# Seven stages in one launch: first inputs loaded in the stage in front, no wait for a stage's own last stores, and another order at the lookup's ends

## The chip, the cores and the metric

One core of one Trainium2 chip runs the whole program in one launch. The metric is the device time in microseconds (us); the reference point is the median of three runs. The engines are TensorE (PE, with its weight loads as PEld), VectorE (DVE), ScalarE (ACT), GpSimd (POOL) and SyncE (SP), which here only issues transfers.

## The reference

Two layers over x of shape (2, 2048, 256) in fp32, 4096 tokens in all. Each of the four blocks is a pre-norm residual block, with `n` a layer norm without weights:

```python
x = x + mamba(n(x))      # norm, W_in (256 to 2x512), causal conv of 4, silu, B, C, delta = softplus(..)
                         # h = exp(delta*A)*h + delta*B*u over time, 16 states x 512 channels
                         # y = sum(h*C) + D*u;  residual + (y * silu(z)) @ W_out
x = x + experts(n(x))    # 16 experts; q,k,v = sum of gated expert projections, causal attention of
                         # one head of 64, its result times each gate, through o_proj
x = x + attention(n(x))  # 16 heads of 16, 4 KV heads, rotary embedding, full softmax over 2048 keys
x = x + lookup(n(x))     # top 8 of 1024 keys, softmax over them, values gathered and weighted,
                         # times a gate from log1p(variance) / mean over all tokens and a small MLP
```

The lookup's gate divides by a mean over all tokens, so no output row can be finished before the last token's variance is known.

## The kernel before

`build_program` (L2398) calls seven stages, one after the other: `mamba_front` (L104), `selective_scan` (L436), `expert_front` (L655, named moe), `causal_attention` (L1050), `rotary_front` (L1285, named rot), `full_attention` (L1542, named attn) and `key_lookup` (L1937, named look). Each opens a Scope with its own tiles and semaphores and a block with one program per engine, written out by hand: an engine runs its list in order and waits on semaphores between. What one stage hands to the next (xr, uT, gT, dT, BC, yT, x1, rwT, qkT, v0, x2, q_parts, k_parts, v1, ctx) goes through tensors in HBM.

All transfers are issued by SP and go through one hardware queue, in the order of SP's program. At the end of its program SP waits until the stage's last stores have landed. Then comes `Scope.clear` (L69): a barrier of all engines, the release of the semaphores, a second barrier. The first transfer of the next stage is issued behind it.

The 4096 tokens are 8 chunks (NCH) of 512 (CH), each of 4 tiles (TPC) of 128; a sequence has 4 chunks (CPB) or 16 tiles (QT).

- **Front.** Per chunk: norms, W_in, conv, silu into uT, the gate silu(z) into gT (ACT L333, L339), B and C rows into xdbl, softplus on ACT and POOL (L235) into dT. uT, gT and dT have one buffer each; SP stores dT of the chunk before, loads x, and stores gT, uT and BC (L153 to L188). After chunk 7 it stores dT once more and waits for all stores.
- **Scan.** SP loads unit 0 (dT, uT; 2 MB), the first quarter of b (rows of B broadcast to 128 partitions, 1 MB each), ident, the C rows, the rest of b, then unit 1. PE transposes the C rows (L630) before anything else. For each of 8 units and 16 states POOL makes du*b (L535), ACT exp(delta*A) (L559), DVE four scan operations (L594), PE and ACT the sum over states. The gated y is stored per unit.
- **moe.** Loads sim, yT, W_out, xr, ident and small inputs, then x1 = xr + y W_out (PE L976), norm, gates, 16 expert projections per chunk (PE L1000), DVE accumulation. Stores x1, rwT, v and qkT.
- **Causal.** SP loads q and k of sequence 0, masks, v, rwB (the gates of a tile of 128 queries broadcast over partitions, two transfers of 256 KB) of unit 0, w_o, rw(1), x of sequence 0, rw(2), rw(3), and all of sequence 1. rwB has 4 buffers; rw(u+4) is issued when unit u is mixed (DVE L1171). Each of 32 units is one tile of queries: scores (PE L1230), mask, softmax, transposes, values, mix with the gates (L1171), w_o and the residual (L1180). x2 is stored every four units.
- **Rot.** Norm of x2 (DVE), transposes (PE L1506), projections (PE L1516), rotary products on DVE, their sum on POOL, a split of q and k into three bf16 parts on ACT, POOL and DVE; stores v1, q_parts, k_parts. DVE does statistics, variance and normalization of a chunk ahead of its turns.
- **Attn.** POOL clears k_max, q, v and sets rows of k_exp to one (L1705 among them), DVE clears k_exp; SP loads parts between these clears. DVE takes maxima (L1787) from products on PE (L1841, L1842), then exp on ACT (L1767), values on PE (L1862). 8 pairs of sequence and KV head, 4 chunks of queries each.
- **Look.** SP loads 16 constants on one semaphore; POOL, DVE, ACT and PE all wait for all 16. PE first multiplies the router weights with the keys (rk), then x3 = x2 + ctx W_o (L2281, DVE L2035), norm, query, router scores, top 8 (MAX8, L2066), weights, `finish` (L2081) after the lookup of the values (PE L2320). `look_all` and `sum_all` hold all tokens. After the last tile DVE computes the variances, ACT Ln, PE the sum over tokens, DVE and ACT the gate (L2251), and DVE 32 results (L2166) in two buffers, which SP stores chunk by chunk (512 KB).

## Time and profile before

| what | value |
| --- | --- |
| median of 3 runs | 3662.48 us (3660.83 to 3666.27) |
| the profiled execution | 3666.12 us, of which the span 3664.1 |
| mean granted TensorE clock | 0.955 of full speed |
| busy in the span | PE 3253.3, DVE 2754.8, ACT 2232.4, POOL 964.0 us |
| transfers | 216.74 MB, mean 59 GB/s |

The stages cover, by their first and last transfers and operations: front 0 to 250, scan 255 to 910, moe 915 to 1357, causal 1360 to 1672, rot 1675 to 1812, attn 1815 to 3283, look 3286 to 3664.

A row of the timeline has the start (us from the span's start), the duration, the engine (SPq is SP's queue), the line, the operation, out<-in, shapes and count; in brackets stands the idle time of that engine before it, and who ended it. Rows of neighbouring operations of one kind are merged, with their count. A row of the windows has the stretch, its length, the busy time of PE, PEld, DVE, ACT and POOL (with counts), the granted clock PEclk, the DMA engines' busy share and the GB/s.

### The profile page before, as it was taken

The numbers are of one execution on the slowest core, as the hardware profiler recorded it, in microseconds if no ns is written. First come the engines' busy times: TensorE is split into PE (matmuls) and PEld (weight loads), VectorE is DVE, ScalarE is ACT, GpSimd is POOL, SyncE is SP. The second block draws the span as 40 slices with busy tenths as digits, with TensorE's granted clock in tenths as the row PEclk, the third lists the DMA queues.
The fourth block names the chain that finished last, engine by engine and source line by source line (L and its number), as shares of the span: only waits on it lengthen the run. The fifth ranks groups of instructions, "written<-read, shape, count | busy, mean of one in ns | idle before, by whom it ended". The sixth has DMA issues, their size and how long they took to land. (4 is left out here: it accounts for less than half of the span.)

```text
span 3664.1 us, 55043 instructions
## 1 busy us (share of the span) xinstructions
PE 3253.3 (89%) x18162; PEld 1625.8 (44%) x18162; DVE 2754.8 (75%) x4130; ACT 2232.4 (61%) x3970; POOL 964.0 (26%) x906
## 2 busy tenths in 40 slices
PE   7848888898899988997789999999999999977896
PEld 3316777776566646774312222222222222214664
DVE  6639999998566653445798888888888888835665
ACT  5659999998100001222258888888888888862442
POOL 7529999997000000002300000000000000001000
PEclk9979999999899998999879999999999999998998
DMA  4448443310311127223300000000000010011001
GB/s 132 166 139 186 124 107 93 104 58 24 107 54 45 44 44 179 70 64 102 103 14 14 21 14 21 14 21 14 21 14 21 16 24 14 9 30 46 23 23 46
DMA packets 218534, 216.74 MB, mean 59 GB/s; under 512 B 63954, under 2 KB 164434, under 8 KB 217492
## 3 DMA queue, kind: packets, MB, share of 16 engines
q1 hardware_dynamic: 218276, 213.41, 21.1%
q8 instruction: 149, 2.44, 0.3%
q14 instruction: 109, 0.89, 0.1%
HBM read 145.99 MB, written 67.37 MB: 58 GB/s over the span
## 5 line engine op out<-in xcount | busy, mean ns | idle before, releaser
L1787 DVE TENSOR_REDUCE attn_part_max<-attn_pM 128x1 f32<-128x1024 f32 x1024 | 1204.9, 1219 | 162.1 <-PE attn_pM L1842 159.0
L1767 ACT ACTIVATE attn_probs<-attn_pE 128x512 f32<-128x512 f32 x2048 | 1089.7, 597 | 205.7 <-PE attn_pE L1891 201.2
L1891 PE MATMUL attn_pE<-attn_q,attn_k_exp 128*128 128x512 bf16 x2048 | 629.0, 385 | 31.3 <-ACT attn_q L1739 24.7
L535 POOL TENSOR_TENSOR scan_dbu<-scan_du,scan_b_all 128x2048 f32<-128x2048 f32 x128 | 578.4, 4553 | 14.9 <-DVE scan_h L594 12.9
L1862 PE MATMUL attn_pA<-attn_probs,attn_v 128*32 128x512 f32 x4096 | 560.3, 604 | 0.0
L594 DVE TENSOR_TENSOR_SCAN scan_h<-scan_abar,scan_states,scan_dbu 128x512 f32<-128x512 f32 x384 | 458.6, 1301 | 0.0
L1891 PEld LDWEIGHTS attn_pE<-attn_q,attn_k_exp 128*128 128x128 bf16 x2048 | 139.1, 97 | 608.7 <-ACT attn_probs L1767 464.6
L608 PE MATMUL scan_hT<-scan_ident,scan_h 128*128 128x128 f32 x2048 | 324.1, 282 | 71.7 <-ACT scan_hcT L546 29.5
L559 ACT ACTIVATE scan_abar<-scan_delta,scan_decay 128x512 f32<-128x512 f32 x512 | 366.8, 717 | 17.3 <-DVE scan_h L594 17.3
L1720 POOL TENSOR_TENSOR attn_peak_parts<-attn_peak,attn_zero 128x4 bf16<-128x4 f32 x128 | 26.6, 208 | 1277.0 <-DVE attn_peak L1791 1277.0
L546 ACT ACTIVATE scan_hcT<-scan_hT,scan_c_t 128x512 f32<-128x512 f32 x512 | 361.7, 707 | 1.1 <-PE scan_hT L608 1.1
L1841 PE MATMUL attn_pM<-attn_k_exp,attn_q 64*128 64x512 bf16 x1024 | 325.9, 391 | 34.4 <-DMA attn_k_exp<-mid_k_parts 18.2
L1000 PE MATMUL moe_pP<-moe_w_qkv,moe_xT 128*128 128x384 f32 x1024 | 339.4, 489 | 0.9
L1842 PE MATMUL attn_pM<-attn_k_max,attn_q 64*128 64x512 bf16 x1024 | 325.9, 391 | 0.0
L618 PE MATMUL scan_y_acc<-scan_ident,scan_hcT 128*128 128x128 f32 x2048 | 303.5, 274 | 1.2 <-DVE scan_g L577 1.0
L608 PEld LDWEIGHTS scan_hT<-scan_ident,scan_h 128*128 128x128 f32 x2048 | 225.2, 143 | 168.7 <-DVE scan_h L594 113.7
L1000 PEld LDWEIGHTS moe_pP<-moe_w_qkv,moe_xT 128*128 128x128 f32 x1024 | 193.0, 191 | 131.3 <-DVE moe_acc L872 4.6
L618 PEld LDWEIGHTS scan_y_acc<-scan_ident,scan_hcT 128*128 128x128 f32 x2048 | 239.8, 142 | 4.6 <-issue 2.5
L1841 PEld LDWEIGHTS attn_pM<-attn_k_exp,attn_q 64*128 64x128 bf16 x1024 | 83.2, 93 | 304.7 <-issue 169.5
L875 DVE SCALAR_TENSOR_TENSOR moe_acc<-moe_pP,moe_rw,moe_acc 128x192 f32<-128x192 f32 x448 | 161.8, 412 | 75.1 <-PE moe_pP L1000 74.5
L594 DVE TENSOR_TENSOR_SCAN scan_h<-scan_abar,scan_dbu 128x512 f32<-128x512 f32 x128 | 150.7, 1221 | 40.5 <-POOL scan_dbu L535 37.7
L1862 PEld LDWEIGHTS attn_pA<-attn_probs,attn_v 128*32 128x32 f32 x4096 | 95.5, 108 | 146.5 <-ACT attn_probs L1767 110.7
(274 smaller groups left out, 3642.8 us busy)
## 6 DMA issues: line engine op xcount, KB each, us to landing
scan_b_all<-mid_BC SPq DMA_DIRECT2D x32, 1024.0 KB, 10.0
causal_rwB<-mid_rwT SPq DMA_DIRECT2D x64, 256.0 KB, 4.2
attn_q<-mid_q_parts SPq DMA_DIRECT2D x224, 64.0 KB, 2.4
mid_gT<-front_gT SPq DMA_DIRECT2D x8, 1024.0 KB, 7.6
mid_uT<-front_uT SPq DMA_DIRECT2D x8, 1024.0 KB, 9.2
mid_dT<-front_dT SPq DMA_DIRECT2D x8, 1024.0 KB, 4.3
scan_delta<-mid_dT SPq DMA_DIRECT2D x8, 1024.0 KB, 8.0
scan_u_in<-mid_uT SPq DMA_DIRECT2D x8, 1024.0 KB, 10.2
```

The lines of the kernel that those rows point to most:

```text
L535: nc.gpsimd.tensor_tensor(dbu[:, G % NDBU, :, :], du[:, u % 2, :, :], b_row, ALU.mult).then_inc(dbu_ready, 1)
L546: nc.scalar.activation(hcT[:, i % NHC, :], hT[:, i % 2, :], ACT.Copy, scale=c_t[:, u * TPC + tile, n:n + 1]).then_inc(hc_ready, 1)
L559: nc.scalar.activation(abar[:, k % 2, :], delta[:, u % 2, m, :], ACT.Exp, scale=decay[:, m, n:n + 1]).then_inc(abar_ready, 1)
L594: nc.vector.tensor_tensor_scan(h[:, G % NH, m, :], abar[:, k % 2, :], dbu[:, G % NDBU, m, :], state, ALU.mult, ALU.add).then_inc(scan_done, 1)
L608: last = nc.tensor.transpose(hT[:, i % 2, m * 128:(m + 1) * 128], h[:, G % NH, m, tile * 128:(tile + 1) * 128], ident[:])
L618: last = nc.tensor.matmul(y_acc[:, m, tile * 128:(tile + 1) * 128], hcT[:, i % NHC, m * 128:(m + 1) * 128], ident[:], start=(n == 0 and ti ...
L1000: last = nc.tensor.matmul(pP[:, n % NP, 0:2 * QKV], xT[:, c % 2, k, j * 128:(j + 1) * 128], w_qkv[:, k, pr * 2 * QKV:(pr + 1) * 2 * QKV], ...
L1767: nc.scalar.activation(probs[:, kt % 4, h, :], pE[:, bank(item), :], ACT.Exp, scale=SCALE).then_inc(exp_done, 1)
L1787: nc.vector.reduce_max(part_max[:, h, j, i:i + 1], pM[:, m % 2, :], AXIS_X).then_inc(max_read, 1)
L1841: nc.tensor.matmul(pM[:, m % 2, 0:CH], q[0:64, qc, h, j * 128:(j + 1) * 128], k_exp[0:64, par, i * CH:(i + 1) * CH], start=True, stop=True)
L1862: last = nc.tensor.matmul(pA[32 * h:32 * h + 32, :], v[:, par, kt, :], probs[:, kt % 4, h, :], start=(kt == 0), stop=(kt == KT - 1))
L1891: nc.tensor.matmul(pE[:, bank(item), :], k_exp[:, par, kt * 128:(kt + 1) * 128], q[:, qc, h, :], start=True, stop=True).then_inc(e_psum, 1)
```

## The change

The first inputs of six of the stages get tiles and semaphores of their own in Scopes (`scan_ahead`, `expert_ahead`, `causal_ahead`, `rotary_ahead`, `attention_ahead`, `lookup_ahead`) that are opened before the stage in front and are passed to both. The stage in front issues their loads.

- Front: at chunk 3 SP waits for three chunks' stores and loads unit 0, a_log and ident; in chunks 4 and 5 it issues two b loads each, ahead of the gT and uT stores. POOL makes du of unit 0 before its last delta. dT is now the scan's odd g tile; the last dT store is waited for in the scan, before gate 1 is loaded into it.
- Scan: starts with the C rows (now in hcT's tile), unit 1, b of unit 1, gate 0, and moe's constants. Its end waits for the even y stores only.
- moe: the first yT and xr come in two halves. At chunk 5 SP waits for the stores of chunks 0 to 4 and issues causal's first loads.
- Causal: SP waits for moe's stores, then loads x, q, k, v of the rest. In unit 17 it issues rot's first loads; DVE does chunk 0's statistics and variance in unit 22 and its normalization in unit 24; POOL the root.
- Rot: clears of attention's tiles on POOL after its add of chunks 0 to 3; attention's loads at chunks 5 and 6. DVE's clear of k_exp is gone from attn, and is POOL's.
- Attn: issues the lookup's constants at its start, and ctx and x2 of the first chunk in its last pair.
- Look: three semaphores for the constants; flips and x3 before the rk product; the gate's chain beside the last lookups, the results of chunks 0 to 3 before the `finish` of tile 30, chunks 4 to 6 before that of tile 31, chunk 7 last, in four buffers.
- No stage but the last waits at its end for its own last stores (the scan for half of them); the next one waits where it reads them.

The core of the diff:

```diff
-    def clear(self):
+    def clear(self, ahead=None):
         self.nc.all_engine_barrier()
-        self.nc.clear_and_free_semaphores(self.sems)
+        self.nc.clear_and_free_semaphores(self.sems + (ahead.sems if ahead else []))
...
+def load_scan_b(sp, a, p, u, i, b):
+    src = a["BC"][i * BQ:(i + 1) * BQ, u * CH:(u + 1) * CH]
+    sp.dma_start(b[:, i * BQ:(i + 1) * BQ, :], src.unsqueeze(0).broadcast_to([128, BQ, CH])).then_inc(p.b_in[u % 2][i], 16)
...
+                    if c == 3:
+                        for sem in (u_out, bc_out):
+                            sp.wait_ge(sem, 16 * c)
+                        sp.wait_ge(d_out, 16 * c)
+                        load_scan_unit(sp, a, following, 0, following.delta_even, following.u_even)
+                        sp.dma_start(following.a_log[:], a["a_log_d"]).then_inc(following.const_in, 16)
+                        sp.dma_start(following.ident[:], a["ident"]).then_inc(following.const_in, 16)
+                    if c in (4, 5):
+                        for i in (2 * c - 8, 2 * c - 7):
+                            load_scan_b(sp, a, following, 0, i, following.b_even)
...
-                for sem in (xr_out, u_out, g_out, bc_out, d_out):
+                for sem in (xr_out, u_out, g_out, bc_out):
...
+                    if c == NCH - 1:
+                        pool.wait_ge(following.unit_in[0], 32)
+                        nc.gpsimd.tensor_tensor(following.du_even[:], following.delta_even[:], following.u_even[:], ALU.mult).then_inc(following.du_ready, 1)
...
+        c_rows = hcT[0:NS, :, :].rearrange("p a c -> p (a c)")
...
-                sp.dma_start(a_log[:], a["a_log_d"]).then_inc(const_in, 16)
-                load_unit(0)
-                load_b(0, 0)
-                sp.dma_start(ident[:], a["ident"]).then_inc(const_in, 16)
+                    load_scan_b(sp, a, p, u, i, b_all[u % 2])
+
                 sp.dma_start(c_rows, BC[NS:2 * NS, :]).then_inc(crow_in, 16)
-                for i in range(1, 4):
-                    load_b(0, i)
                 load_unit(1)
                 for i in range(4):
                     load_b(1, i)
-                sp.wait_ge(c_psum, 1)
                 load_gate(0)
+                load_expert_ahead(sp, a, following)
+                sp.wait_ge(p.d_out, 16 * NCH)
                 load_gate(1)
                 for u in range(UNITS):
...
+                sp.wait_ge(y_out[0], UNITS // 2 * 16)
...
+def load_causal_ahead(sp, a, p):
+
+    load_qk(sp, a, p, 0)
+    sp.dma_start(p.above[:], a["above"]).then_inc(p.above_in, 16)
+    sp.dma_start(p.ident[:], a["ident"]).then_inc(p.ident_in, 16)
+    load_v(sp, a, p, 0)
+    for u in range(NRW):
+        load_rw(sp, a, p, u)
+    sp.dma_start(p.w_o[:], a["w_o"].rearrange("(m p) n -> p m n", p=128)).then_inc(p.w_in, 16)
...
+                for half, arrived in enumerate((first_in, y_in)):
+                    sp.dma_start(yT[:, :, half * 256:(half + 1) * 256], yT_view[:, :, half * 256:(half + 1) * 256]).then_inc(arrived, 16)
+                    sp.dma_start(xr[:, 2 * half:2 * half + 2, :], xr_view[:, 2 * half:2 * half + 2, :]).then_inc(arrived, 16)
...
+                        if c + 2 == NCH - 1:
+                            sp.wait_ge(p.y_out[1], 16 * NCH // 2)
                         load_y(c + 2)
+                    if c == CPB + 1:
+                        sp.wait_ge(qk_out, 16 * c)
+                        sp.wait_ge(rw_out, 16 * (c + 1))
+                        for par in range(2):
+                            sp.wait_ge(v_out[par], 16 * ((c + 1 - par) // 2))
+                        load_causal_ahead(sp, a, following)
                     store_v(c)
                 store_qk(NCH - 1)
-                for sem in (x1_out, qk_out, rw_out):
-                    sp.wait_ge(sem, 16 * NCH)
-                for sem in v_out:
-                    sp.wait_ge(sem, 16 * NCH // 2)
...
+                for sem in (p.x1_out, p.qk_out, p.rw_out):
+                    sp.wait_ge(sem, 16 * NCH)
+                for par in range(2):
+                    sp.wait_ge(p.v_out[par], 16 * NCH // 2)
                 load_x(0)
-                load_rw(2)
-                load_rw(3)
-                load_qk(1)
-                load_v(1)
+                load_qk(sp, a, p, 1)
+                load_v(sp, a, p, 1)
                 load_x(1)
                 for u in range(UNITS):
                     if u + NRW < UNITS:
-                        load_rw(u + NRW)
+                        sp.wait_ge(mix_ready, u + 1)
+                        load_rw(sp, a, p, u + NRW)
+                    if u == QT + 1:
+                        sp.wait_ge(x_out, 16 * QUARTERS)
+                        load_rotary_ahead(sp, a, following)
                     b, qt = divmod(u, QT)
                     n = QT // QUARTERS
                     if qt % n == n - 1:
                         sp.wait_ge(x_ready, u + 1)
                         sp.dma_start(x2_view[:, u + 1 - n:u + 1, :], x[:, b, qt + 1 - n:qt + 1, :]).then_inc(x_out, 16)
-                sp.wait_ge(x_out, 16 * QUARTERS * B)
+
+            @block.gpsimd
+            def _(pool):
...
+                nc.gpsimd.memset(following.mhalf[:], -0.5).then_inc(following.half_set, 1)
+                pool.wait_ge(following.half_set, 1)
+                rotary_root(nc, pool, following, 0)
...
+                    if u == QT + 6:
+                        rotary_statistics(nc, dve, following, 0)
+                        rotary_variance(nc, dve, following, 0)
+                    if u == QT + 8:
+                        rotary_normalize(nc, dve, following, 0)
                     if u:
                         add(u - 1)
...
+def clear_attention_ahead(nc, pool, p, turn):
+
+    if turn == 0:
+        nc.gpsimd.memset(p.k_max[64:128, :, :].bitcast(FP32), 0.0).then_inc(p.kmax_clear, 1)
+        pool.wait_ge(p.kmax_clear, 1)
+        nc.gpsimd.memset(p.v[:], 0.0).then_inc(p.v_clear, 1)
+        pool.wait_ge(p.v_clear, 1)
+    elif turn == 1:
+        nc.gpsimd.memset(p.q[PEAK:128, :, :, :].bitcast(FP32), 0.0).then_inc(p.q_clear, 1)
+        pool.wait_ge(p.q_clear, 1)
+    elif turn == 2:
+        nc.gpsimd.memset(p.k_exp[64:128, :, :].bitcast(FP32), 0.0).then_inc(p.kexp_clear, 1)
+        pool.wait_ge(p.kexp_clear, 1)
+    else:
+        nc.gpsimd.memset(p.k_exp[PEAK:PEAK + PARTS, :, :], 1.0).then_inc(p.ones_set, 1)
+        pool.wait_ge(p.ones_set, 1)
+        nc.gpsimd.memset(p.v[:, :, :, HW:HW + 1], 1.0).then_inc(p.ones_set, 1)
+        pool.wait_ge(p.ones_set, 2)
...
+                sp.wait_ge(p.x_out, 16 * NCH)
                 for c in range(NCH):
                     if c + 2 < NCH:
                         sp.wait_ge(xh_ready, (c + 1) * TPC)
-                        load_x(c + 2)
+                        load_rotary_x(sp, a, p, c + 2)
+                    if c == CPB + 1:
+                        for par in range(2):
+                            sp.wait_ge(v_out[par], 16 * CPB // 2)
+                            sp.wait_ge(parts_out[par], 16 * NOUT * CPB // 2)
+                        load_attention_maxima(sp, a, following)
+                    if c == CPB + 2:
+                        load_attention_rest(sp, a, following)
...
+                    if c < CPB:
+                        pool.wait_ge(q_ready, (c + 1) * NPC)
+                        clear_attention_ahead(nc, pool, following, c)
...
+                for par in range(2):
+                    sp.wait_ge(p.v_out[par], 16 * NCH // 2)
+                    sp.wait_ge(p.parts_out[par], 16 * 2 * PARTS * NCH // 2)
+                load_lookup_ahead(sp, a, following)
...
+                        if last and qc == 1:
+                            sp.wait_ge(ctx_out, 16 * (u - 1))
+                            load_lookup_x(sp, a, following, 0)
...
+                sp.wait_ge(p.ctx_out, 16 * NCH * NKV)
+                with sp.Fori(1, NCH) as c:
                     sp.wait_ge(x3_ready, c * TPC)
...
+                    load_lookup_x(sp, a, p, c)
+                for c in range(NCH):
+                    sp.wait_ge(out_ready, (c + 1) * TPC)
+                    sp.dma_start(out_view[:, c * TPC:(c + 1) * TPC, :], result[:, c % 4, :, :]).then_inc(out_done[c % 4], 16)
+                for sem in out_done:
+                    sp.wait_ge(sem, 16 * (NCH // 4))
...
+                def results(c):
+                    dve.wait_ge(look_ready, (c + 1) * TPC)
+                    if c >= 4:
+                        dve.wait_ge(out_done[c % 4], 16)
+                    for j in range(TPC):
+                        n = c * TPC + j
+                        nc.vector.scalar_tensor_tensor(result[:, c % 4, j, :], look_all[:, n, :], gate[:, n:n + 1], sum_all[:, n, :], ALU.mult, ALU.add).then_inc(out_ready, 1)
...
-                marks = body(NCH - 1, 0, marks)
                 ch = Chain(dve, dve_sem, marks)
-                ch.wait()
...
+                variances(ch)
+                n, first = NT - TPC, ch.n
+                weigh(n + 1, 1)
+                pick(n + 2, 0, marks + ch.n)
+                finish(n, 0)
+                ch.n += TILE_MARKS
+                weigh(n + 2, 0)
+                pick(n + 3, 1, marks + ch.n)
+                ch.n += TILE_MARKS
+                gate_input(ch)
+                finish(n + 1, 1)
+                weigh(n + 3, 1)
                 dve.wait_ge(gate_ready, 1)
...
+                for c in range(NCH // 2):
+                    results(c)
+                finish(n + 2, 0)
+                for c in range(NCH // 2, NCH - 1):
+                    results(c)
+                finish(n + 3, 1)
+                results(NCH - 1)
...
-                body(NCH - 1, 0, 0)
+                n = NT - TPC
+                move_weights(n)
                 act.wait_ge(var_all, 1)
                 nc.scalar.activation(logv[:], var_v[:], ACT.Ln, bias=1.0, accum_out=tmp_v[:, 0:1]).then_inc(lsum_ready, 1)
                 act.wait_ge(learn_ready, NCH)
                 nc.scalar.activation(gate[:], learned_all[:], ACT.Sigmoid, bias=scalars[:, 0:1]).then_inc(unc_ready, 1)
+                expo(n + 2, 0)
+                move_weights(n + 1)
+                expo(n + 3, 1)
+                move_weights(n + 2)
                 act.wait_ge(unc_ready, 2)
                 nc.scalar.activation(gate[:], gate[:], ACT.Sigmoid, bias=scalars[:, 2:3], scale=scalars[:, 1:2]).then_inc(gate_ready, 1)
+                move_weights(n + 3)
...
-                pe.wait_ge(w_in, 16 * NW)
-                pe.wait_ge(const_set, 2)
+                pe.wait_ge(o_in, 16 * O_LOADS)
+                flip_ctx(0)
+                x3_pair(0, 0)
+                x3_pair(0, 1)
+                pe.wait_ge(x3_ready, TPC)
+                pe.wait_ge(q_in, 16 * Q_LOADS)
                 for i in range(2):
                     nc.tensor.matmul((pX, pL)[i][:], w_r[:], keysT[:, i * CH:(i + 1) * CH], start=True, stop=True).then_inc(rk_psum, 1)
-                flip_ctx(0)
+                flip_xh(0)
                 pe.wait_ge(rk_moved, 2)
...
-                flip_xh(0)
                 project(0, TPC)
                 route(0)
+                pe.wait_ge(rest_in, 16 * REST_LOADS)
...
+                    if not ahead:
+                        pe.wait_ge(const_set, 2)
+                        pe.wait_ge(lsum_ready, 1)
+                        pe.wait_ge(learn_ready, NCH)
+                        nc.tensor.matmul(pX[:, 0:1], ones[:], tmp_v[:, 0:1], start=True, stop=True).then_inc(lsum_psum, 1)
```

## Rows read from the trace of the kernel before

**Rows 1.** Timeline, SP's queue: the last store of six stages, and lookup's first load.

```profile
249.77 0.36 SPq L160 DMA_DIRECT2D mid_dT<-front_dT  x1
...
910.16 0.36 SPq L513 DMA_DIRECT2D mid_yT<-scan_g  x1
...
1356.76 0.33 SPq L729 DMA_DIRECT2D mid_qkT<-moe_qkT  x1
...
1671.61 0.38 SPq L1142 DMA_DIRECT2D mid_x<-causal_x  x1
...
1811.25 0.51 SPq L1335 DMA_DIRECT2D mid_k_parts<-rot_part  x1
...
3282.84 0.37 SPq L1660 DMA_DIRECT2D mid_ctx<-attn_ctx  x1
...
3286.17 0.35 SPq L1996 DMA_DIRECT2D look_ident<-in_ident  x1
```

**Rows 2.** DMA issues of the whole run: KB each, median us to landing.

```profile
scan_b_all<-mid_BC SPq DMA_DIRECT2D x32, 1024.0 KB, 10.0
...
mid_dT<-front_dT SPq DMA_DIRECT2D x8, 1024.0 KB, 4.3
...
mid_ctx<-attn_ctx SPq DMA_DIRECT2D x32, 128.0 KB, 2.0
```

**Rows 3.** Timeline: the first main operation behind each edge; idle time before in brackets.

```profile
274.02 3.56 PE L630 MATMUL scan_hT<-scan_ident,scan_g 16*128 16x16 f32 x32 [37.36 <-DMA scan_g<-mid_BC]
...
278.97 3.45 DVE L594 TENSOR_TENSOR_SCAN scan_h<-scan_abar,scan_dbu 128x512 f32<-128x512 f32 x3 [1.44 <-ACT scan_abar L559]
...
924.68 5.88 PE L976 MATMUL moe_pX<-moe_w_out,moe_yT 128*128 128x256 f32 x13 [5.77 <-DMA moe_xr<-mid_xr]
...
1370.56 0.79 PE L1230 MATMUL causal_pS<-causal_kT,causal_qT 64*128 64x128 f32 x2 [14.46 <-DMA causal_kT<-mid_qkT]
...
1684.89 1.94 PE L1506 MATMUL rot_pT<-rot_ident,rot_xh 128*128 128x128 f32 x8 [13.83 <-DVE rot_xh L1405]
...
1825.85 9.14 DVE L1787 TENSOR_REDUCE attn_part_max<-attn_pM 128x1 f32<-128x1024 f32 x8 [1.39 <-PE attn_pM L1842]
...
3310.11 0.76 DVE L2035 TENSOR_TENSOR look_x<-look_pX,look_x 128x256 f32<-128x256 f32 x2 [2.09 <-PE look_pX L2281]
```

**Rows 4.** Windows: the lookup's start, and a stretch of full attention.

```profile
3311.00:3332.00 21.00, 13.52 (x30) 5.39 (x30) 6.92 (x21) 5.06 (x8) 3.37 (x2) 0.59 0.17 50
2100.00:2500.00 400.00, 392.00 (x2491) 97.56 (x2490) 349.68 (x343) 334.71 (x631) 30.62 (x144) 1.00 0.07 18
```

**Rows 5.** Timeline, front: gT's store of chunk 4, and ACT's next write of it.

```profile
148.26 1.11 SPq L184 DMA_DIRECT2D mid_gT<-front_gT  x1
...
168.99 2.06 ACT L333 ACTIVATE front_gT<-front_pXZ 128x512 f32<-128x512 f32 x4
```

**Rows 6.** Timeline, causal attention, DVE: the two waits for transfers.

```profile
1390.85 0.48 DVE L1180 SCALAR_TENSOR_TENSOR causal_x<-causal_pO,causal_rsum,causal_x 128x256 f32<-128x256 f32 x1 [5.13 <-DMA causal_x<-mid_x]
...
1418.23 1.22 DVE L1171 TENSOR_TENSOR causal_mixedT<-causal_pA,causal_rwB 128x1024 f32<-128x1024 f32 x1 [11.62 <-DMA causal_rwB<-mid_rwT]
```

**Rows 7.** Timeline, rotary, PE: first projections and late ones.

```profile
1688.10 9.06 PE L1516 MATMUL rot_pP<-rot_xT,rot_w_qk 128*128 128x512 f32 x16 [1.27 <-ACT rot_xT L1472]
...
1794.45 10.66 PE L1516 MATMUL rot_pP<-rot_xT,rot_w_qk 128*128 128x512 f32 x24
```

**Rows 8.** Timeline, start of full attention: POOL and DVE side by side.

```profile
1820.87 3.51 POOL L1705 MEMSET attn_k_exp<- 3x4096 bf16 x1
1820.90 3.56 DVE L1803 CAST attn_ident_bf<-attn_ident 128x128 bf16<-128x128 f32 x1 [3.36 <-DMA attn_ident<-in_ident]
```

**Rows 9.** Timeline, ACT, in the lookup's end.

```profile
3625.48 1.09 ACT L2173 ACTIVATE look_weightT<-look_pT 128x512 f32<-128x512 f32 x2 [0.92 <-PE look_pT L2258]
...
3640.09 0.42 ACT L2251 ACTIVATE look_gate<-look_gate,look_scalars 128x32 f32<-128x32 f32 x1 [0.55 <-DVE look_gate L2157]
```

**Rows 10.** Lines, 3611 to 3664: busy us, mean ns, idle before and its releasers.

```profile
L2166 DVE SCALAR_TENSOR_TENSOR look_result<-look_look_all,look_gate,look_sum_all 128x256 f32 x32 | 13.0, 480 | 6.4 <-DMA out<-look_result 5.5 <-ACT look_gate L2251 0.9
```

625 lines of the change are left out of this document (323 added, 302 removed).

## The prediction, made before the result

> **What bounds the kernel now.** I read first where each stage stops issuing transfers and where the next one starts to compute, then the transfers' landing times, the clock, and the last stage's end. The seven stages run strictly one after the other. At each of the six edges the sync queue issues its last store [rows 1], waits until it has landed (2.0 us for ctx, 4.3 us for the 1 MB dT, [rows 2]), passes the barrier, and only then asks for the next stage's inputs, which take some 10 us more. The reader should see in [rows 3] what the first operation behind each edge waits for: c_rows for 37 us, kT/qT for 14.5 us, the normalized x for 13.8 us. From last store to first real work it is 29.2, 14.5, 13.8, 13.3, 14.6 and 27.3 us: 113 us in which no engine does the kernel's main work. The barrier is worth 1.3 us: the ctx store is issued at 3282.84, lands 2.0 later, and the next stage's first transfer goes out at 3286.17 [rows 1, 2]. Inside the stages the engines are full (TensorE 392 of 400 us in attention, at full clock, [rows 4]), and the change leaves those inner loops alone. So it is worth what it takes from the edges, from two stalls inside causal attention, and from the end of the lookup.
>
> **The sum, part by part**, against the profiled execution's 3666.1 us (span 3664.1 and 2.0 around it). It stands 3.6 above the median.
>
> *Front to scan.* The front ends at its last dT store (249.77, issue over by 250.1); with 1.3 of barrier the c_rows load goes out at 251.4. It queues behind that 1 MB store, so I let it land about 256.5 (255.5 to 258). The c transposes (3.56), their copy and one abar operation (1.44 of wait before the third scan operation) follow: the third scan operation starts at about 261 instead of 278.97 [rows 3]. Unit 0, b and du are there already. **+18.0** (16 to 18.6).
>
> *What the early loads cost the front.* 2 MB of unit 0 at chunk 3, and two broadcast b loads ahead of the gT/uT stores in chunks 4 and 5. Their price beside the front's traffic isn't in the trace: a plain 1 MB transfer lands in 4.3 us, a broadcast one in 10.0 in the scan's crowd [rows 2]. gT's store of chunk 4 is issued at 148.26, and ACT writes that tile again at 168.99 [rows 5]. With 4.3 each, the two loads and the store are through at 161.2, in time. With 10.0 for each load and 4.3 to 10.0 for the store it is 172.6 to 178.3, 3.6 to 9.3 late; about 7.5 with uT behind it, and again a chunk later: 15. I take **−1.5** (0 to −15), near the plain end, since the front's queue is emptier than the scan's. The du product lies in an idle stretch of POOL ahead of its last delta and costs nothing.
>
> *Scan to expert front.* Last yT store 910.16, 1.3 of barrier, then half of yT and half of xr (0.75 MB at about the dT price, 4.3) instead of the whole of both behind sim and w_out: first product at about 917 instead of 924.68. **+7.7** (6 to 9).
>
> *Expert front to causal.* q, k, v, the first rw and the weights are loaded in chunk 5. Last qkT store 1356.76, barrier, scores at 1358.6 instead of 1370.56: **+12.0**. In the first units the waits for v, rwB, w_o and for x (5.13 at 1390.85, [rows 6]) shrink, since 7 MB instead of 12.5 MB pass the queue: **+3.3** (0 to 6). The same crowd makes DVE wait 11.62 us for rwB of unit 4 at 1418.23 [rows 6]; SP now issues that load only behind 5 MB, and by those bytes it lands near the time when it is needed. I count **+9.5** of the 11.6 (0 to 11), the rest being work that PE has in that gap. Added in units 22 and 24: statistics, variance and normalization of the next stage's first chunk on DVE: eight operations of 128x256, at most 0.48 us each by the one of that shape in [rows 6], and seven tiny ones, some 4 us. DVE waits for x or PE in every unit there, so **−0.3** (0 to −4).
>
> *Causal to rotary.* Last x2 store 1671.61; xh is ready before the stage ends, so the transposes start at 1672.9 instead of 1684.89: **+12.0**. They and the first projections ran at half clock: 16 matmuls in 9.06 us, 0.57 each, against 24 in 10.66, 0.44 each, later [rows 7]; that is 2 us, and the transposes half a us. With a gap of 2 instead of 14 us the clock should stay: **+2.5** (0 to 3).
>
> *Memsets moved into rotary.* POOL clears attention's tiles behind its add in chunks 0 to 3. In the old place one of 4096 elements takes 3.51 us [rows 8]; by elements (12,352 in six) they make 10.6. POOL has room: **−1** (0 to −10.6). The far end comes from the row beside it: a cast of only 128x128 on DVE, begun 0.03 us later, took 3.56 us and ended with the memset, so DVE can stand still for a whole memset. Most of rotary's DVE operations have other operands than a cast, so I stay near the low end.
> The Trainium skill (SBUF — State Buffer, "SBUF: two separate sides") has a rule that speaks against this step: VectorE and GpSimd share a port pair under an exclusive lock, and the loser is blocked for the other's whole instruction; against a GpSimd operation that reads nothing from SBUF, as a memset, this holds for VectorE's two-port modes. The trace agrees in its one case. By the rule each memset that meets such an operation costs its full length, and the term could be −10.6.
>
> *Rotary to attention.* Last k_parts store 1811.25, barrier, first maxima at 1813.85 instead of 1825.85 (q, k, v there, the DVE memset of k_exp gone): **+12.0** (11 to 12.5). The first maxima are DVE's, so the clock adds 0 to 2 there; I count none.
>
> *Attention to lookup.* Last ctx store 3282.84. The lookup's constants lie ready, also ctx and x2 of its first chunk; the product of router weights and keys moves behind x3. Barrier to 3284.5, POOL's bias, flips 1.4 and two pairs: the second pair's add ends at about 3293.3 instead of 3310.87 [rows 3]: **+17.6** (15 to 18). From 3311 to 3332 the clock was 0.59 with PE busy 13.5 of 21 us [rows 4]. At 1.00 that work would take 13.5 × 0.59 = 8.0, so 5.5 at most comes back; part of it isn't on the path: **+3.4** (0 to 5.5).
>
> *The lookup's end.* Before: after the last lookup come variance, Ln and two Sigmoids, the gate at 3640.09+0.42, then 32 results: 13.0 us of work with 6.4 of waiting, of which 5.5 for output buffers [rows 9, 10]. Ends 3659.5. After: the gate's chain runs beside the last lookups. ACT's move for tile 30 ends at 3626.6 [rows 9]; the Ln, Sigmoid and Exp put ahead of it make it some 1 us later, and with a table load and the last Sigmoid (0.42) the gate is ready at about 3629.5. 16 results (0.41 each) end at 3636.0, then a finish of about a result's length, 12 results to 3641.4, the last finish, and 4 results to 3643.5; with four buffers none waits. **+15.9** (13 to 17).
>
> **Sum**: gains 18.0+7.7+12.0+3.3+9.5+12.0+2.5+12.0+17.6+3.4+15.9 = 113.9, costs 1.5+0.3+1.0 = 2.8: 111.1 less. 3666.1 becomes 3555.0 for an execution like the profiled one, and 3551.4 from the median. I say **3552**.
>
> A second place where a page and a row differ. A broadcast b load of 1 MB lands in 10.0 us, a plain store of the same size in 4.3 [rows 2]. The Trainium skill (DMA: Bandwidth & Descriptors, "Anatomy of one DMA") fits, for transfers issued by GpSimd, 2.0 us plus the bytes at 436 GB/s, which makes an estimate of 4.4 us for either; by it the front would lose nothing and the sum would be 112.6. The row of the b loads is far above that; since a landing time holds the wait behind earlier transfers too, it does not settle what one costs in the front, and both ends stay in the range.
>
> **Rivals.**
> *B, the early b loads hold the front.* For: 10.0 us landing, and ACT has no spare buffer for gT and uT. Against: at 4.3 each all three fit between store and rewrite, with 7.8 us to spare. The full 15 instead of 1.5: 3565.
> *C, the rw(4) stall stays.* For: SP must still wait for unit 0's mix before this load, behind 5 MB. Against: those 5 MB start 12 us earlier relative to the work. 9.5 more: 3561.
> *D, the ends still cost the landing*, so that the change doesn't do what it says: something at the barrier waits for the stores all the same (2.0 to 4.3 us at six edges, 18 in all): 3570. Against: no wait on those stores is left before the barrier, but for the scan's even y stores, which land a unit earlier.
> *L, the memsets block DVE in rotary*, as one did the cast: 9.6 more, 3561. Against: the cast's operands are not those of rotary's products, and DVE has waits there.
> *E, slower than before: the clock doesn't hold.* TensorE now has no pauses of 14 us; if the chip answers with a lower grant in attention, PE is its bound (392 of 400 us busy at 1.00, [rows 4]). The stage has some 1440 us; 111 us are gone once the mean grant is 0.928. At 0.90 it costs 160: 3712. Against: the grant is 1.00 through the 400 us shown, where PE never pauses for long, and the low grant of 0.59 stands behind an idle edge, not behind work.
>
> **How the numbers follow.** The forecast (each term near its value) 0.52, B 0.12, C 0.13, L 0.08, D 0.06, other sums of small misses 0.05, E 0.04. The range takes in B, C, L and D's lower part, singly or two together, and below it the terms' good ends (clock at attention, the x stalls: 13 less): 3538 to 3578. A measurement of this kernel tells about 0.2% (7 us) from no change; all cases but E are far beyond it. Faster 0.95, same 0.01, slower 0.04.
>
> **What would show it.** Last store to first work under 3 us at causal, rotary and attention, about 7 at the expert front, 11 at the scan and at the lookup's add; the front's last store within 2 us of 249.8 (B: 256 or more, with ACT idle before gT at chunks 5 and 6); no DVE wait of over 2 us for rwB at unit 4; rotary as long as before from first transpose to last store (L: 5 to 10 us longer, with small DVE operations of some 3.5 us); clock 1.00 at rotary's and the lookup's start; results of the lookup without waits for out. I would be wrong if the inner parts of the scan or attention, which the diff leaves as they are, became longer.

## The result, and the profile after

The changed kernel takes 3566.97 us (median of 4 runs, 3561.59 to 3571.08) against 3662.53 (4 runs, 3660.83 to 3666.27) before, run in turn on the same chip: a ratio of 0.9737, with a 95% interval of 0.972 to 0.9754. The forecast was 3552, in a range of 3538 to 3578. The profiled execution after took 3561.59 us, 104.5 less than the profiled one before (3666.12). The medians differ by 95.6 only; the first experiment below is about those 9 us.

From the page of the profile after, span and first engine row:

```profile
span 3559.8 us, 54793 instructions
...
PE 3222.1 (91%) x17996; PEld 1622.3 (46%) x18162; DVE 2750.6 (77%) x4129; ACT 2234.5 (63%) x3972; POOL 965.3 (27%) x907
```

PE's busy time is 31 us lower than before, but most of that is in the records and not in the work. 25 us lie in full attention (1404.8 us before, 1379.5 after), where this profile lacks 166 matmul records; the profile of finish_early below has them all, and 1406.1 us there. Some 6 us lie in causal attention (271.1 us, now 265.2), where less ran at half clock (mean grant 0.95, now 0.98). The busy times of DVE, ACT and POOL differ by less than 5 us.

The timeline of the kernel after, in order: the last store of a stage on SP's queue, and the first main operation of the next. These lines answer to [rows 1] and [rows 3].

```profile
252.66 0.36 SPq L192 DMA_DIRECT2D mid_dT<-scan_g_odd  x1
...
254.53 0.33 SPq L552 DMA_DIRECT2D scan_hcT<-mid_BC  x1
...
265.22 3.45 DVE L648 TENSOR_TENSOR_SCAN scan_h<-scan_abar,scan_dbu 128x512 f32<-128x512 f32 x3 [3.64 <-ACT scan_abar L613]
...
895.39 0.36 SPq L569 DMA_DIRECT2D mid_yT<-scan_g_odd  x1
...
903.14 5.57 PE L1149 MATMUL moe_pX<-moe_w_out,moe_yT 128*128 128x256 f32 x16 [4.62 <-DMA moe_xr<-mid_xr]
...
1335.04 0.33 SPq L898 DMA_DIRECT2D mid_qkT<-moe_qkT  x1
...
1336.95 0.68 PE L1389 MATMUL causal_pS<-causal_kT,causal_qT 64*128 64x128 f32 x2 [2.57 <-PEq L72]
...
1621.79 0.38 SPq L1291 DMA_DIRECT2D mid_x<-causal_x  x1
...
1623.85 1.94 PE L1699 MATMUL rot_pT<-rot_ident,rot_xh 128*128 128x128 f32 x8 [2.60 <-PEq L72]
...
1750.39 0.51 SPq L1564 DMA_DIRECT2D mid_k_parts<-rot_part  x1
...
1753.76 9.14 DVE L1975 TENSOR_REDUCE attn_part_max<-attn_pM 128x1 f32<-128x1024 f32 x8 [0.75 <-PE attn_pM L2029]
...
3211.21 0.42 DVE L1987 TENSOR_TENSOR attn_ctx<-attn_o_cols,attn_inv 128x256 f32<-128x256 f32 x1
...
3223.57 0.76 DVE L2200 TENSOR_TENSOR look_x<-look_pX,look_x 128x256 f32<-128x256 f32 x2 [2.09 <-PE look_pX L2471]
```

Read the brackets first. At causal's and rotary's start nothing waits for a transfer any more: PEq L72 is the barrier in `Scope.clear`. From last store to first work it is now 12.6, 7.8, 1.9, 2.1 and 3.4 us, against 29.2, 14.5, 13.8, 13.3 and 14.6. For the lookup both profiles are counted from attention's last DVE operation: now the second add starts 12.4 us behind it, and before 27.7, from this row of the kernel before:

```profile
3282.39 0.42 DVE L1799 TENSOR_TENSOR attn_ctx<-attn_o_cols,attn_inv 128x256 f32<-128x256 f32 x1
```

The whole difference of the two profiled spans, each place by two rows before and two after, and the terms of the prediction beside it (us gained):

| place | predicted | measured |
| --- | --- | --- |
| front, to its last store | -1.5 | -2.9 |
| edge to the scan | 18.0 | 16.6 |
| inside the scan | 0 | 1.0 |
| edge to the expert front | 7.7 | 6.8 |
| inside the expert front | 0 | 0.2 |
| edge to causal | 12.0 | 11.9 |
| inside causal (3.3 + 9.5 - 0.3) | 12.5 | 16.2 |
| edge to rotary | 12.0 | 11.2 |
| inside rotary (2.5 - 1.0) | 1.5 | -0.2 |
| edge to attention | 12.0 | 11.2 |
| inside attention | 0 | -0.9 |
| edge to the lookup's second add | 17.6 | 15.4 |
| from there to its first top 8 | 3.4 | 3.8 |
| the rest of the lookup, its end | 15.9 | 13.9 |
| sum | 111.1 | 104.2 |

Inside causal the waits of DVE are read from the lines of the kernel after, 1337 to 1640 (busy us, mean ns, idle before and who ended it). DVE's mix waits 1.5 us for rwB in the whole stage; the same group of the kernel before had 19.4, of which [rows 6] show the 11.62. First before, then after:

```profile
L1171 DVE TENSOR_TENSOR causal_mixedT<-causal_pA,causal_rwB 128x1024 f32<-128x1024 f32 x32 | 39.2, 1225 | 58.2 <-PE causal_pA L1253 30.9 <-DMA causal_rwB<-mid_rwT 19.4 <-ACT causal_probs L1202 8.0
...
L1325 DVE TENSOR_TENSOR causal_mixedT<-causal_pA,causal_rwB 128x1024 f32<-128x1024 f32 x32 | 39.2, 1224 | 43.3 <-PE causal_pA L1412 31.4 <-ACT causal_probs L1361 10.3 <-DMA causal_rwB<-mid_rwT 1.5
```

And the lookup's end, DVE and PE in the timeline of the kernel after; it answers to [rows 9, 10]:

```profile
3539.53 6.42 DVE L2272 SCALAR_TENSOR_TENSOR look_result<-look_look_all,look_gate,look_sum_all 128x256 f32<-128x256 f32 x16 [1.84 <-ACT look_gate L2440]
3545.88 0.47 DVE L2246 TENSOR_SCALAR look_look_all<-look_pL,look_winv 128x256 f32<-128x256 f32 x1
3546.27 4.82 DVE L2272 SCALAR_TENSOR_TENSOR look_result<-look_look_all,look_gate,look_sum_all 128x256 f32<-128x256 f32 x12
3553.16 0.48 DVE L2246 TENSOR_SCALAR look_look_all<-look_pL,look_winv 128x256 f32<-128x256 f32 x1 [2.06 <-PE look_pL L2510]
3553.68 1.67 DVE L2272 SCALAR_TENSOR_TENSOR look_result<-look_look_all,look_gate,look_sum_all 128x256 f32<-128x256 f32 x4
...
3546.50 6.55 PE L2510 MATMUL look_pL<-look_values,look_weightT 128*128 128x256 f32 x16 [4.08 <-DVE look_look_all L2246]
```

No result waits for a store. A new wait is there instead: PE's last lookup needs the PSUM tile that `finish(30)` frees, this finish stands behind 16 results, PE idles 4.08 us, and then works at half clock (6.55 us for what took 3.72 in the profile of finish_early).

### The profile page after: what moved, and what is told of

It reads as the page before. It is cut to its first block and busy times, and to the rows that moved or that the text cites. A ratio compares the mean times of both kernels' runs of the same rounds, so it can differ in the third digit from the quotient of the medians.

```text
span 3559.8 us, 54793 instructions
## 1 busy us (share of the span) xinstructions
PE 3222.1 (91%) x17996; PEld 1622.3 (46%) x18162; DVE 2750.6 (77%) x4129; ACT 2234.5 (63%) x3972; POOL 965.3 (27%) x907
## 5 line engine op out<-in xcount | busy, mean ns | idle before, releaser
L2078 PE MATMUL attn_pE<-attn_q,attn_k_exp 128*128 128x512 bf16 x1882 | 590.5, 385 | 54.6 <-ACT attn_q L1927 24.7
L589 POOL TENSOR_TENSOR scan_dbu<-scan_du_odd,scan_b_odd 128x2048 f32<-128x2048 f32 x64 | 289.7, 4557 | 8.9 <-DVE scan_h L648 8.9
L589 POOL TENSOR_TENSOR scan_dbu<-scan_du_even,scan_b_even 128x2048 f32<-128x2048 f32 x64 | 289.2, 4553 | 7.3 <-DVE scan_h L648 5.2
L613 ACT ACTIVATE scan_abar<-scan_delta_even,scan_decay 128x512 f32<-128x512 f32 x256 | 188.9, 738 | 7.9 <-DVE scan_h L648 7.9
L613 ACT ACTIVATE scan_abar<-scan_delta_odd,scan_decay 128x512 f32<-128x512 f32 x256 | 182.7, 714 | 8.5 <-DVE scan_h L648 8.5
```

The lines of the kernel that those rows point to most:

```text
L589: nc.gpsimd.tensor_tensor(dbu[:, G % NDBU, :, :], du[u % 2][:], b_row, ALU.mult).then_inc(dbu_ready, 1)
L613: nc.scalar.activation(abar[:, k % 2, :], delta[u % 2][:, m, :], ACT.Exp, scale=decay[:, m, n:n + 1]).then_inc(abar_ready, 1)
L2078: nc.tensor.matmul(pE[:, bank(item), :], k_exp[:, par, kt * 128:(kt + 1) * 128], q[:, qc, h, :], start=True, stop=True).then_inc(e_psum, 1)
```

## Experiments

All are edits of the changed kernel. Times are medians; "before" is the kernel before, timed in turn with them on the same chip (3666.05, 3664.57 and 3666.78 us in the three groups of kernels). Comparisons between two edits of different groups are no better than some 3 us.

### control: the changed kernel again

```diff
(no edit)
```

> The changed kernel again, nothing edited. Its profiled execution took 3561.6 us, its four runs 3561.6 to 3571.1 (median 3567.0), against 3662.5 before: 104.5 us by the two profiled executions, 95.6 by the medians. If the 104 us that the trace accounts for are what the change is worth, the median here lies near 3562; if other executions lose some 5 us more, it lies near 3567 again with a spread of 8 us or more, and the profile shows where (I expect places where the granted clock is at half).

3567.26 us (5 runs, 3562.21 to 3569.46), ratio to before 0.9724 (0.9711 to 0.9738). The profiled execution's span is 3566.4, 6.6 more than in the first profile. By the same rows as above, causal is 1.7 longer, rotary with its edge 0.9 shorter, attention 2.0 longer, the lookup 3.7 longer. Windows of the lookup, from its first top 8 to its last results, first of the changed kernel's first profile, then of control:

```profile
3242.00:3554.00 312.00, 270.93 (x1244) 194.12 (x1244) 208.39 (x510) 122.25 (x168) 23.33 (x13) 0.94 0.10 32
```

```profile
3245.00:3561.00 316.00, 276.29 (x1246) 199.16 (x1244) 208.69 (x511) 122.36 (x169) 23.40 (x13) 0.92 0.10 32
```

The same work keeps PE busy 5.4 us longer, at a mean grant of 0.92 instead of 0.94; DVE's and ACT's busy times are equal. In windows of 2 us the clock is at half once or more in most chunks of the lookup, and for how long (from none to 8 us at the same place) differs from one execution to the next. So the first profile of the changed kernel was a fortunate execution (the fastest of its four), and that of before (3666.12) was slower than three of its kernel's four runs: the 104 us that the traces account for are 95 to 99 by medians. What made attention 2.0 us longer stays open.

The profiles of this section show how much a stage varies where nothing in it was edited, and everything below has to be read against that. The front's last store stands anywhere from 252.6 to 255.7 in the ten kernels that leave the front's loads as they are. Attention takes 1456.5 to 1459.6 us, and the lookup from its first top 8 to its last result 312.1 to 316.8.

### end_waits: the stages wait for their own last stores again

```diff
-                for sem in (xr_out, u_out, g_out, bc_out):
+                for sem in (xr_out, u_out, g_out, bc_out, d_out):
...
                 sp.wait_ge(y_out[0], UNITS // 2 * 16)
+                sp.wait_ge(y_out[1], UNITS // 2 * 16)
...
+                for sem in (x1_out, qk_out, rw_out):
+                    sp.wait_ge(sem, 16 * NCH)
+                for sem in v_out:
+                    sp.wait_ge(sem, 16 * NCH // 2)
...
+                sp.wait_ge(x_out, 16 * QUARTERS * B)
...
+                for par in range(2):
+                    sp.wait_ge(v_out[par], 16 * NCH // 2)
+                    sp.wait_ge(parts_out[par], 16 * NOUT * NCH // 2)
...
+                sp.wait_ge(ctx_out, 16 * NB * QC)
```

> Every stage waits at its end for its own last stores again, as before the change; all early loads stay. Theory (the landing is on the path, 2.0 to 4.3 us at each of six edges): 12 to 18 us slower than control, the gap between last store and first work at rotary's start 5 us instead of 2.1. Rival (the landing was hidden behind the barrier, and the gain came from the early loads alone): within 3 us of control.

3582.47 us (5 runs), 15.2 slower than control: the theory holds, inside its 12 to 18 us. The edge to rotary in this kernel's timeline:

```profile
1632.46 0.38 SPq L1296 DMA_DIRECT2D mid_x<-causal_x  x1
...
1637.05 1.94 PE L1708 MATMUL rot_pT<-rot_ident,rot_xh 128*128 128x128 f32 x8 [5.15 <-PEq L72]
```

The gap is 4.6 us against 2.1. Over the six edges the gaps are longer than control's by 2.8, 2.3, 1.7, 2.5, 1.5 and 3.4 us, 14.2 in all. (At the last one 1.8 of the 3.4 is clock: DVE waits 3.88 us for the second pair of x3 products there, in control 2.09.) So of the 77 us gained at the edges (with the lookup to its first top 8) some 12 to 14 come from not waiting for the landing, and the rest from the early loads and the order behind them. This rest is by subtraction: no kernel here takes back the early loads of an edge, but for rw_here inside causal.

### b_behind: the four early b loads behind the chunk's stores

```diff
-                    if c in (4, 5):                  # ahead of the gT store
-                        for i in (2 * c - 8, 2 * c - 7):
-                            load_scan_b(sp, a, following, 0, i, following.b_even)
...
                     sp.dma_start(a["BC"][:, c * CH:(c + 1) * CH], xdbl[DTR:DTR + 2 * NS, :]).then_inc(bc_out, 16)
+                    if c in (4, 5):
+                        for i in (2 * c - 8, 2 * c - 7):
+                            load_scan_b(sp, a, following, 0, i, following.b_even)
```

> The four early loads of b in the front are issued behind the chunk's gT, uT and BC stores instead of ahead of them. Theory (the 2.9 us that the front lost are the stores of gT and uT landing late, so that ACT waits for its tile): the front's last dT store goes back from 252.66 to 250.3 or earlier (0.5 us may stay with du on POOL), the whole 2 to 3 us faster than control. Rival (the queue is full either way, and the next chunk's dT store and x load are late instead): the last dT store stays at 252 or later.

The front's last store goes back to 250.43, nearly as far as the theory has it (250.3), and clear of the 252.6 to 255.7 of the other kernels. In the changed kernel ACT could be seen to wait for the store of its gT tile at chunk 5, which [rows 5] show free of a wait; timeline of the kernel after:

```profile
169.07 1.28 ACT L378 ACT_TABLE_LOAD   x1 [1.42 <-DMA mid_gT<-front_gT]
```

In b_behind ACT has no such wait. The whole took 3566.5 us, 0.8 less than control, which can't be told from no change: of the 2.2 us, 1.6 are gone by the scan's last y store (894.68, against 895.25 in control).

### rw_here: rwB and w_o loaded in causal again

```diff
-    for u in range(NRW):
-        load_rw(sp, a, p, u)
-    sp.dma_start(p.w_o[:], a["w_o"].rearrange("(m p) n -> p m n", p=128)).then_inc(p.w_in, 16)
...
+                load_rw(sp, a, p, 0)
+                sp.dma_start(w_o[:], a["w_o"].rearrange("(m p) n -> p m n", p=128)).then_inc(w_in, 16)
+                load_rw(sp, a, p, 1)
                 load_x(0)
+                load_rw(sp, a, p, 2)
+                load_rw(sp, a, p, 3)
```

> rwB of units 0 to 3 and w_o are loaded at the start of causal attention, in the old order, instead of in the stage in front. Theory (the crowd in the queue at causal's start made its stalls): DVE waits 8 us or more for rwB again (1.5 us in the changed kernel, 19.4 before) and the whole is 10 to 17 us slower than control. Rival (the early q, k and v alone relieve the queue): under 4 us slower.

3583.4 us (4 runs), 16.1 slower than control: theory. The lines of DVE in causal, and the two largest waits in its timeline:

```profile
L1327 DVE TENSOR_TENSOR causal_mixedT<-causal_pA,causal_rwB 128x1024 f32<-128x1024 f32 x32 | 39.2, 1224 | 56.3 <-PE causal_pA L1414 30.5 <-DMA causal_rwB<-mid_rwT 17.2 <-ACT causal_probs L1363 8.7
```

```profile
1359.52 0.48 DVE L1336 SCALAR_TENSOR_TENSOR causal_x<-causal_pO,causal_rsum,causal_x 128x256 f32<-128x256 f32 x1 [6.34 <-DMA causal_x<-mid_x]
...
1386.31 1.22 DVE L1327 TENSOR_TENSOR causal_mixedT<-causal_pA,causal_rwB 128x1024 f32<-128x1024 f32 x1 [9.90 <-DMA causal_rwB<-mid_rwT]
```

The stall at unit 4 is back with 9.90 us and x's with 6.34, and causal is 14.2 us longer than in control. So what removed them is the 3 MB of rwB and w_o taken out of the crowd, and the gain inside causal is a matter of the queue, not of the edge.

### memset_twice: POOL's clears in rotary doubled

```diff
+        nc.gpsimd.memset(p.q[PEAK:128, :, :, :].bitcast(FP32), 0.0).then_inc(p.extra, 1)
+        pool.wait_ge(p.extra, 3)
         nc.gpsimd.memset(p.q[PEAK:128, :, :, :].bitcast(FP32), 0.0).then_inc(p.q_clear, 1)
```

(the same for the other four large ones)

> Each of the five large clears that POOL does in rotary is done twice: 10.7 us more of memsets (0.95, 0.96, 3.51, 1.80, 3.51). Theory (POOL's room there hides them, and they hold no DVE operation of rotary): from first transpose to last k_parts store 126.5 us as in the changed kernel, within 0.7. Rival (a memset blocks DVE for its whole length, as it did the cast of the kernel before): 5 to 11 us more, and DVE operations of about 3.5 us in the trace.

3582.34 us (4 runs), 15 slower than control. Rotary, from first transpose to last store, took 136.95 us. The first profile has 126.54 and control 125.67. Control is the one to compare with, since its first transposes ran at full clock (1.06 us), as they did here. So it is 11.3 more: the rival. POOL and DVE in this kernel's timeline:

```profile
1663.71 3.51 POOL L1502 MEMSET attn_q<- 32x4096 f32 x1
1667.27 3.51 POOL L1504 MEMSET attn_q<- 32x4096 f32 x1
```

```profile
1667.14 0.16 DVE L766 TENSOR_TENSOR rot_var<-rot_st 128x4 f32<-128x4 f32 x1
1667.33 3.48 DVE L767 TENSOR_SCALAR rot_st<-rot_st 128x4 f32<-128x4 f32 x1
1667.41 3.40 DVE L768 TENSOR_TENSOR rot_st<-rot_st 128x4 f32<-128x4 f32 x1
1667.49 3.33 DVE L769 TENSOR_SCALAR rot_var<-rot_var 128x4 f32<-128x4 f32 x1
1670.89 0.16 DVE L770 SCALAR_TENSOR_TENSOR rot_var<-rot_st,rot_var 128x4 f32<-128x4 f32 x1
```

A TENSOR_SCALAR over four elements per partition lasts from just behind the second memset's start until that memset ends (1667.27 + 3.51 = 1670.78), and everything behind it on DVE stands: the TENSOR_TENSOR and the second TENSOR_SCALAR in these rows end with it. The TENSOR_TENSORs, SCALAR_TENSOR_TENSORs and statistics that DVE did beside the first memset are as short as ever. It happens at the second clear of q and at the second setting of k_exp's rows of ones, 3.3 us each, and for 0.2 us at the end of v's. PE then waits for DVE, and its clock falls. The transposes of five chunks in this kernel:

```profile
1656.48 1.09 PE L1710 MATMUL rot_pT<-rot_ident,rot_xh 128*128 128x128 f32 x8 [1.55 <-DVE rot_xh L778]
...
1674.63 1.97 PE L1710 MATMUL rot_pT<-rot_ident,rot_xh 128*128 128x128 f32 x8 [4.63 <-DVE rot_xh L778]
...
1691.19 1.09 PE L1710 MATMUL rot_pT<-rot_ident,rot_xh 128*128 128x128 f32 x8 [1.42 <-DVE rot_xh L778]
...
1709.34 1.97 PE L1710 MATMUL rot_pT<-rot_ident,rot_xh 128*128 128x128 f32 x8 [4.63 <-DVE rot_xh L778]
...
1727.29 1.09 PE L1710 MATMUL rot_pT<-rot_ident,rot_xh 128*128 128x128 f32 x8 [1.41 <-DVE rot_xh L778]
```

The first chunk that is hit comes 18.15 us after the one before it, where an undisturbed period in control is 14.95, and the next one 16.56 us later, since the chunk began at half clock (1.97 us for what takes 1.09): 4.8 us for this held operation. The second costs 6.2 (18.15 and 17.95), since the clock stays at half for 6 us there and for 3 at the first. Together they are 11.0 of the 11.3. Of the whole's 15 us, 3.1 more stand at the front's last store (255.73), which the edit doesn't touch.

### clear_swapped: the same clears, in another place

```diff
     elif turn == 1:
+        nc.gpsimd.memset(p.k_exp[64:128, :, :].bitcast(FP32), 0.0).then_inc(p.kexp_clear, 1)
+        pool.wait_ge(p.kexp_clear, 1)
         nc.gpsimd.memset(p.q[PEAK:128, :, :, :].bitcast(FP32), 0.0).then_inc(p.q_clear, 1)
         pool.wait_ge(p.q_clear, 1)
-    elif turn == 2:
-        nc.gpsimd.memset(p.k_exp[64:128, :, :].bitcast(FP32), 0.0).then_inc(p.kexp_clear, 1)
-        pool.wait_ge(p.kexp_clear, 1)
-    else:
+    elif turn == 3:
```

> The same clears once each, but the zeroing of k_exp (1.80 us) stands in chunk 1 ahead of that of q (3.51 us) instead of in chunk 2. In the profile of the repeated changed kernel q's clear ends 0.12 us before DVE's first TENSOR_SCALAR of the statistics; here it ends 1.8 us later. Theory (a memset holds only those DVE operations that are of TENSOR_SCALAR's kind, for its rest): that TENSOR_SCALAR takes about 1.8 us instead of 0.17, and rotary, from first transpose to last k_parts store, 1 to 2 us more. Rival (the 10 us of the doubled clears came from POOL's own lateness, its add or root behind the clears): no TENSOR_SCALAR over 0.3 us, and rotary under 0.5 us longer.

POOL and DVE in its timeline:

```profile
1664.77 3.51 POOL L1499 MEMSET attn_q<- 32x4096 f32 x1
```

```profile
1666.53 1.77 DVE L767 TENSOR_SCALAR rot_st<-rot_st 128x4 f32<-128x4 f32 x1
```

1.77 us, and 1666.53 + 1.77 = 1668.30, with the memset ending at 1668.28. Rotary took 127.06 us, 1.4 more than control's 125.67, which began at full clock as this one did. (The first profile's 126.54 began at half clock.) With not one instruction more, the theory holds for the operation to a few hundredths of a us, and for the stage it is inside its 1 to 2 us. The whole took 3571.63 (4 runs, ratio 0.9736, 0.972 to 0.9752), which can't be told from control's ratio.

### finish_early: finish(30) behind 8 results

```diff
-                for c in range(NCH // 2):
-                    results(c)
-                finish(n + 2, 0)
-                for c in range(NCH // 2, NCH - 1):
+                for c in range(NCH - 1):
+                    if c == 2:
+                        finish(n + 2, 0)
                     results(c)
```

> At the lookup's end the finish of tile 30 stands behind 8 results instead of behind 16. Theory (TensorE's last lookup waits for the PSUM tile that this finish frees: it waited 4.08 us, and took 6.55 us at half clock instead of 3.72): the lookup of tile 31 starts 2.5 to 3 us earlier, DVE's 2.06 us wait before the finish of tile 31 goes, 2 us faster than control. Rival (the stores of the results set the end): no change.

The lookup of tile 31 in its timeline:

```profile
3547.75 3.72 PE L2509 MATMUL look_pL<-look_values,look_weightT 128*128 128x256 f32 x16 [1.23 <-ACT look_weightT L2357]
```

3.72 us at full clock, DVE doesn't wait for it, and from the first result to the start of the last four it is 12.0 us instead of 14.3 in control. The theory's 2 us are there in the trace, and in rows that the edit touches. The whole took 3563.52 (5 runs), ratio 0.9726 (0.9713 to 0.9739): below control by 3.7 us, above it by the ratio; a gain of 2 us is too small for these runs.

### c_late: ACT copies the C rows later

```diff
+                    if k == LAG - 1:
                         act.wait_ge(c_psum, 1)
                         nc.scalar.activation(c_t[:].rearrange("p t n -> p (t n)"), hT[:, 1, :], ACT.Copy).then_inc(c_ready, 1)
```

> In the scan ACT copies the transposed C rows behind its sixth abar operation instead of behind its second. Theory (the 5.7 us landing of the C rows holds only ACT's copy, and the scan operations stand behind it by ACT's order alone): the third scan operation starts 3 to 3.6 us earlier, at 261.6 instead of 265.2, and the whole is about 3 us faster than control. Rival (the h tiles or the turns of h hold DVE a few operations later, and give it back): first y no earlier, under 1 us.

DVE's first scan operations in its timeline:

```profile
260.27 5.69 DVE L649 TENSOR_TENSOR_SCAN scan_h<-scan_abar,scan_dbu 128x512 f32<-128x512 f32 x5 [18.90 <-POOL scan_dbu L589]
```

The third operation follows the second at once; counted from the front's last store, the sixth starts 12.3 us later and in control 15.9: 3.6 us are gained there. But DVE now waits for POOL's product (21.6 us in the stage instead of 18.9), and from the front's last store to the last y store the stage is 1.2 us shorter, not 3: the rival. The whole, 3565.65 us, is 1.6 below control, within the noise. POOL's first products (4.5 us each), by these waits, are the next bound there; no run tests that.

### tail_old: the lookup's end in the old order, with four buffers

```diff
+                marks = body(NCH - 1, 0, marks)
                 ch = Chain(dve, dve_sem, marks)
                 variances(ch)
-                n, first = NT - TPC, ch.n
...
                 gate_input(ch)
...
                 dve.wait_ge(gate_ready, 1)
-                for c in range(NCH // 2):
+                for c in range(NCH):
                     results(c)
```

(and ACT's and PE's programs to match)

> The lookup's end in the old order: last chunk whole, then variances, Ln, sum, gate, then all 32 results; the four result buffers stay. The new order and buffers together gave 14.5 us by the first profile, of which 5.5 are waits for two buffers in the profile of before. Theory: 9 us slower than control by the trace (from the top 8 of tile 0 to the last result), and no wait for a store among the results. Rival (the four buffers brought nothing, since the stores are slower than the results): the waits come back, 14 us slower.

3574.89 us, 7.6 slower than control; from the first top 8 to the end of the results 324.75 us against 316.54, 8.2 more (11.6 more than in the first profile; the clock's scatter lies between). The results in its timeline:

```profile
3557.18 12.76 DVE L2272 SCALAR_TENSOR_TENSOR look_result<-look_look_all,look_gate,look_sum_all 128x256 f32<-128x256 f32 x32 [0.48 <-ACT look_gate L2421]
```

32 results in one run, no wait for a store. So the order is worth some 8 us, and the buffers the 5.5 of waiting in [rows 10].

### rk_first: the product of router weights and keys first again

```diff
                 pe.wait_ge(o_in, 16 * O_LOADS)
-                flip_ctx(0)
-                x3_pair(0, 0)
-                x3_pair(0, 1)
-                pe.wait_ge(x3_ready, TPC)
                 pe.wait_ge(q_in, 16 * Q_LOADS)
                 for i in range(2):
                     nc.tensor.matmul((pX, pL)[i][:], w_r[:], keysT[:, i * CH:(i + 1) * CH], start=True, stop=True).then_inc(rk_psum, 1)
+                flip_ctx(0)
+                pe.wait_ge(rk_moved, 2)
+                x3_pair(0, 0)
+                x3_pair(0, 1)
                 flip_xh(0)
-                pe.wait_ge(rk_moved, 2)
```

> The lookup begins with the product of router weights and keys again, ahead of flips and x3; all its inputs are there early. Theory (15.4 us of the edge come from the loads, little from the order): the second add starts 4 to 6 us later than in control, but the top 8 of tile 0 only 1 to 3 us later, since the product and its copies have to be made in either order. Rival (the order is worth its full product): top 8 of tile 0 5 us later.

Both sizes were off. From attention's last operation the second add comes after 13.5 us (12.7 in control), and the first top 8 after 36.0 (31.3): 0.9 and 4.6 us later. The 4.6 can't be put down to the order. What stands between is at half clock here (four matmuls of w_u 3.65 us, in control 1.90), and clear_swapped, whose lookup is not edited, has its first top 8 after 35.9 us too, with the same 3.65 us for w_u. Its second add:

```profile
3230.58 0.76 DVE L2199 TENSOR_TENSOR look_x<-look_pX,look_x 128x256 f32<-128x256 f32 x2 [3.83 <-PE look_pX L2470]
```

By the last result the difference to control is 0.2 us (348.0 and 347.9 us from attention's last operation), but to the first profile (344.1) it is 3.9: the rest of the lookup happened to have the better clock here and in the first profile. The whole, 3566.28, with its ratio of 0.9726, is not told apart from control's. The 0.9 us at the second add could be clock too (13.9 us there in clear_swapped). So the order at the lookup's start is worth nothing that can be measured; its edge, 27.7 us before, is gained by the loads.

### best: three edits together

The edits of b_behind, c_late and finish_early in one kernel.

> b loads behind the front's stores, the C copy late, and the finish of tile 30 behind 8 results, together. If the three are independent (2.2, 3 and 2 us) the profile's sum is 7 us below control's and the ratio to before about 0.971 to 0.970; the b loads alone gave 0.6 us by the medians, since the scan gave 1.6 of the 2.1 back.

3562.45 us (5 runs, 3558.18 to 3566.76), ratio 0.9724 (0.971 to 0.9737). That is 4.8 below control by medians and equal to it by the ratio: it beats the kernel before, and is not told apart from the changed one. In its trace each of the three is there (last dT store at 249.90, no wait at the third scan operation, the last lookup 3.72 us).

## Why the prediction was right, and where it was off

**The place of the gain.** Right: 77 us came at the six edges and the lookup's start, where 82.7 were predicted, and no engine became a new bound inside a stage. Rival D fell: its waits put back by hand cost 15.2 us, against the 18 of its price.

**The total alone would not have shown this.** 3567 lies inside the range, but 15 us above the forecast and near the numbers of the rivals B (3565) and D (3570). It is the rows, and the two kernels end_waits and b_behind, that rule these out. One miss upwards (3.7 us in causal) also covers part of the misses downwards. Of the signs that the prediction named, three did not come: the front's last store moved by 2.9 us and not by 2 or less, the scan's gap was 12.6 and not 11, and the clock was at half at rotary's and the lookup's start.

**The barrier's 1.3 us.** Too small. With no landing to wait for, last store to first work is 1.9 to 2.1 us where all inputs are ready. Rotary's and attention's edges were each reckoned 0.8 us too short by it, and that is why they gained 11.2 and not 12.0. Causal's, reckoned with 1.8 us, gained 11.9.

**Edge to the scan, 18.0.** 16.6 came. Counted from the front's last store, the C rows were issued at 1.9 instead of 1.6 us, PE started on them at 7.6 (260.26, 5.7 us behind the issue) instead of 6.7, and the third scan operation followed 5.0 us later instead of 4.5; [rows 3] have 4.95 for this last step (274.02 to 278.97). So the landing "about 256.5" was 0.6 us short, and the chain behind it 0.5. c_late shows further that the term's chain (rows, transposes, copy, abar) held the third operation by ACT's order alone, and that waits for POOL's products take its place for 2.7 us.

**What the early loads cost the front, -1.5.** It was -2.9 in the first profile, between the plain end and rival B's 15, and -2.8 to -6.0 over the ten kernels with these loads. b_behind gives 2.2 of it back at the front's end and almost nothing at the kernel's. The estimate from the Trainium skill (DMA: Bandwidth & Descriptors, "Anatomy of one DMA"), by which the loads would cost nothing, was too low: the 1.42 us wait for gT's store stands in the trace. The four b loads landed after 14.8 us there (median), above both ends of the prediction's 4.3 to 10.0, and gT's store of chunk 4, issued behind two of them, after 18.5.

**Inside causal, 12.5.** 16.2 came, the largest miss upwards. I had counted 9.5 of the stall at unit 4 and 3.3 for the rest; rwB's waits fell by 17.9 us in all and x's by 5.1, to nothing, and rw_here puts 14 us back into the stage. Rival C fell: the load for unit 4 landed with 1.5 us of waiting left (1.49 before the fifth mix, at 1367.87). The statistics and the normalization that were moved in are not visible as a loss.

**Causal to rotary, clock 2.5.** It did not come: this is the step whose mechanism failed. "With a gap of 2 instead of 14 us the clock should stay" is not what the rows show. The first transposes took 1.94 us as before, so the clock was at half although PE had paused for 2.60 us only, and the grant was 0.50 from 1623.85 to 1629.85. In control the same transposes, behind the same pause, took 1.06 us, and rotary was 0.9 us shorter:

```profile
1625.51 1.06 PE L1699 MATMUL rot_pT<-rot_ident,rot_xh 128*128 128x128 f32 x8 [2.60 <-PEq L72]
```

But there the grant fell right behind them, to 0.50 from 1627.50 to 1633.50. So the short gap was followed by some 6 us of half clock in both executions, and only where they began differs. Nor is it chance at this pause alone: of the eleven profiles with the 2.60 us pause, five have about 1.9 us for the transposes and six have 1.06. All five of the first kind have a causal stage of 284.8 to 284.9 us, and none of the second is below 286.4. Why the two go together stays open.

**Memsets in rotary, -1 (0 to -10.6).** The measured loss is nil (126.36 us before, 126.54 after, both begun at half clock), but not for the first reason given: "POOL has room" is not what hides them. The second, that most of rotary's DVE operations have other operands than a cast, is right as far as it goes. The two experiments show that a memset holds a DVE operation of TENSOR_SCALAR's kind for the rest of its length, and the statistics have two of that kind in each chunk. Rival L's mechanism is there; it costs nothing here because no such operation falls beside a clear, by 0.12 us in control. Its timeline, POOL's clear of q (which ends at 1663.85) and the statistics' first TENSOR_SCALAR:

```profile
1660.34 3.51 POOL L1497 MEMSET attn_q<- 32x4096 f32 x1
```

```profile
1663.97 0.17 DVE L767 TENSOR_SCALAR rot_st<-rot_st 128x4 f32<-128x4 f32 x1
```

The rule of the Trainium skill (SBUF — State Buffer, "SBUF: two separate sides") agrees with these traces: the held operation is blocked until the memset ends, not slowed, and TENSOR_TENSORs, which read two SBUF operands, went on beside a memset, which reads none (0.16 us each).

**Lookup.** The edge gave 15.4 of 17.6: flips and first x3 products ran partly at half clock, 3.78 us for eight matmuls of x3, where 1.99 is the later time; that is 1.8 of the 2.2 missing. The clock term was 3.8 against 3.4. The end gave 13.9 of 15.9: the gate came as worked out (the first result 297.4 us behind the first top 8, 297.1 reckoned), and the missed step is "the last finish": its lookup waits for a PSUM tile that the first finish frees, 2.06 us on DVE, which finish_early removes.

**The total.** The terms miss 7 us (111.1 against 104.2 by the traces). The other 8 of the 15 between 3552 and 3567 are in how single executions stand to medians: I took the profile of before as 3.6 above its median, but the profile after lies 5.4 below its own. Rival E fell: attention's own mean grant is 0.98 where it was 0.99, and attention took 0.9 us more, against the 111 that would have been needed. Over the whole span the mean grant rose from 0.955 to 0.970.

## What to carry to other kernels

Price an edge between stages from two rows, the last store and the first real operation behind it; the wait for the landing was some 14 us over six such edges here, and most of the rest was loads asked for too late. A memset that GpSimd does "in its idle time" is free only if no VectorE operation that it can hold falls beside it: look at the kinds and times of the neighbours, not at the busy share. And a sum made against one profiled execution is only as good as that execution's place among its runs: here 3.6 us above the median before and 5.4 below it after. The same goes for an edit judged by a stage's length in two profiles: look first at what an unedited kernel does there.

## What the runs showed that was not expected

- A 128x4 TENSOR_SCALAR on DVE took 3.48 us and 1.77 us beside a GpSimd memset of 3.51 us, each time ending with the memset, where it takes 0.17 us alone; TENSOR_TENSOR, SCALAR_TENSOR_TENSOR and BATCH_NORM_STATS2 beside the same memset kept their times.
- Two DVE operations, each held for 3.3 us, cost their stage 4.8 and 6.2 us, since PE's pause behind them (4.63 instead of 1.43 us) was followed by half clock for some 3 and some 6 us.
- A pause of TensorE of 2.60 us stood before eight transposes at half clock (1.94 us) in one execution, and at full clock (1.06 us) in another of the same kernel, where the clock fell right behind them.
- The mean grant in the lookup was 0.94 in one execution and 0.92 in another of the same kernel, worth 5.4 us of PE's busy time and 3.3 us of the stage.
- The lookup's first top 8 came 31.3 and 35.9 us behind attention's last operation in two kernels whose lookups are the same (control and clear_swapped): as much as the edit of rk_first seemed to cost.
